# Cross-attention in one kernel: the transpose of the score maxima moved from the middle of a step to its end, the scores moved behind the output projection's first chunks

## What is computed

```python
q = split_heads(x @ Wq.T)            # 20 heads of 32
k = split_heads(ctx @ Wk.T)
v = split_heads(ctx @ Wv.T)
scores = einsum('bhsd,bhld->bhsl', q, k) / sqrt(32)
out = merge_heads(einsum('bhsl,bhld->bhsd', softmax(scores), v))
return out @ Wo.T + bo + x
```

## Time and profile before

| | |
|---|---|
| runs | 435.67 us median (434.54 to 435.75) |
| profiled execution | 436.16 us, of which the span in the profile is 434.4 us |
| TensorE matmul (PE) | busy 426.1 us, 98%, 2538 instructions |
| TensorE weight load (PEld) | 313.9 us, 72% |
| GpSimd (POOL) | 300.5 us, 69% |
| ScalarE (ACT) | 253.9 us, 58% |
| VectorE (DVE) | 232.7 us, 54% |
| chain of waits | PE 94%, POOL 2%, ACT 1%, DVE 1%, issue 1% |
| DMA | 72.68 MB, mean 167 GB/s |

### The profile page before, as it was taken

One profiled execution on the slowest core, in us unless ns is written; L12 is line 12 of the kernel. 1 busy time (PEld: TensorE's weight loads), 2 busy tenths in 40 slices (PEclk: granted clock), 3 DMA queues, 4 the chain that ended last, 5 costly groups with the idle time before them and its releaser, 6 DMA issues.

```text
span 434.4 us, 8258 instructions
## 1 busy us (share of the span) xinstructions
PE 426.1 (98%) x2538; PEld 313.9 (72%) x2538; DVE 232.7 (54%) x437; ACT 253.9 (58%) x509; POOL 300.5 (69%) x256
## 2 busy tenths in 40 slices
PE   8999999899999999999999999999999999999996
PEld 6977765677777777777777677777777677777675
DVE  0354766455545555555544555555554455555553
ACT  1737987657465755748464755757564755754510
POOL 8427799989568765959658674959658674955540
PEclk9999999899999999999999999999999999999999
DMA  8997545443455345543355335543355334444203
GB/s 288 359 351 230 203 135 196 146 146 127 145 191 174 122 151 205 205 146 123 135 186 190 123 130 206 204 166 123 125 195 189 124 121 150 157 157 146 75 24 121
DMA packets 39614, 72.68 MB, mean 167 GB/s; under 512 B 5024, under 2 KB 6176, under 8 KB 39584
## 3 DMA queue, kind: packets, MB, share of 16 engines
q1 hardware_dynamic: 28784, 52.62, 34.2%
q10 hardware_dynamic: 10800, 19.67, 14.0%
HBM read 28.81 MB, written 10.49 MB: 90 GB/s over the span
## 4 chain that ended last, share of the span: by engine, by line
PE 94%; POOL 2%; ACT 1%; DVE 1%; issue 1%; DMA 0%; POOLq 0%; ACTq 0%
PE ps_q L673 30%; PE ps_o L673 27%; PE ps_s L731 10%; PE ps_pv L738 7%; PE ps_m L717 5%; PE ps_den L743 4%; PE ps_o L656 2%; POOL p_lo L334 1%; PE ps_m L784 1%; PE ps_s L643 1%; PE ps_m L722 1%; PE ps_q L784 1%; PE ps_q L635 1%; DVE x_f L578 1%; PE ps_o L784 1%
## 5 line engine op out<-in xcount | busy, mean ns | idle before, releaser
L334 POOL TENSOR_TENSOR p_lo<-p_f,p_hi 77x512 f16<-77x512 f32 x160 | 183.2, 1166 | 99.8 <-ACT p_hi L432 97.8
L428 ACT ACTIVATE p_f<-ps_s 77x512 f32<-77x512 f32 x160 | 94.7, 592 | 47.6 <-PE ps_s L731 47.6
L548 DVE TENSOR_REDUCE mx<-ps_m 128x4 f32<-128x308 f32 x160 | 69.3, 475 | 57.7 <-PE ps_m L717 57.4
L432 ACT ACTIVATE p_hi<-ps_s 77x512 f16<-77x512 f32 x160 | 93.5, 584 | 3.0 <-PE ps_den L743 3.0
L541 DVE TENSOR_TENSOR q_lo<-ps_q,q_hi 128x512 fp32r<-128x512 f32 x40 | 27.7, 692 | 101.8 <-ACT q_hi L414 101.8
L673 PE MATMUL ps_q<-x_hi,wq_hi 128*128 128x512 f32 x200 | 79.4, 397 | 0.2 <-POOL wq_lo L348 0.2
L673 PE MATMUL ps_q<-x_lo,wq_hi 128*128 128x512 f32 x200 | 78.3, 391 | 0.0
L673 PE MATMUL ps_q<-x_hi,wq_lo 128*128 128x512 f32 x200 | 78.2, 391 | 0.0
L673 PE MATMUL ps_o<-attn_hi,wo_hi 128*128 128x512 f32 x170 | 70.0, 411 | 0.0
L673 PE MATMUL ps_o<-attn_hi,wo_lo 128*128 128x512 f32 x170 | 67.4, 397 | 0.0
L673 PE MATMUL ps_o<-attn_lo,wo_hi 128*128 128x512 f32 x170 | 67.4, 396 | 0.0
(11 more groups left out here) (105 smaller groups left out, 522.1 us busy)
## 6 DMA issues: line engine op xcount, KB each, us to landing
q_packed<-q_hi SPq DMA_DIRECT2D x80, 256.0 KB, 2.5
x_f<-in_x SPq DMA_DIRECT2D x40, 256.0 KB, 3.3
q_packed<-q_lo SPq DMA_DIRECT2D x40, 256.0 KB, 3.2
x_res<-in_x ACTq DMA_DIRECT2D x35, 256.0 KB, 2.7
out<-out_sb ACTq DMA_DIRECT2D x35, 256.0 KB, 2.6
wk_sb<-in_wk SPq DMA_DIRECT2D x8, 320.0 KB, 5.4
wv_sb<-in_wv SPq DMA_DIRECT2D x5, 512.0 KB, 5.9
wq_sb<-in_wq SPq DMA_DIRECT2D x5, 320.0 KB, 5.6
```

Of the source, the lines that this page charges most:

```text
L334: nc.gpsimd.tensor_tensor(p_lo[:, i, :], p_f[:, i, :], p_hi[:, i, :], ALU.subtract).then_inc(plo_done, 1)
L428: nc.scalar.activation(p_f[:, i, :], ps_s[i % 2][0:L, :], ACT.Exp, scale=SCALE).then_inc(pf_done, 1)
L432: nc.scalar.activation(p_hi[:, i, :], ps_s[i % 2][0:L, :], ACT.Exp, scale=SCALE).then_inc(phi_done, 1)
L548: nc.vector.tensor_reduce(mx[:, g % RS, :, tt], ps_m[tt % 2][:, 0:HG * L].rearrange("p (h k) -> p h k", k=L), AX_X, ALU.max).then_inc(max_ ...
```

## The change

On TensorE, in all steps behind the filling ones, the order within a step is another. Before: values, scores of heads 0 and 1, two maxima matmuls, output chunks 0 and 1, two maxima matmuls, score 2, output chunks 2 and 3, score 3, transpose of the maxima, output chunk 4, the five query chunks. After: values, two maxima matmuls, output chunks 0 and 1, two maxima matmuls, output chunk 2, scores 0 and 1, output chunks 3 and 4, score 2, query chunk 0, score 3, query chunks 1 to 4, transpose of the maxima. The filling steps stay as they were.

On ACT the copy of the maxima (`copy_max`), and on SP the transfer of them (`load_max`), move from the step that transposes them to the start of the next one. Nothing is added or removed.

```diff
@@ SP, step
-                if exists(shift(t, g, 1)[0]):
+                if exists(t) and not filling(*shift(t, g, -1)):
+                    load_max(t, g)
+                if filling(t, g) and exists(shift(t, g, 1)[0]):
                     load_max(*shift(t, g, 1))
@@ ACT, step
                 xt, (at, chunks) = x_split_at(t, g), attn_split_at(t, g)
+                if exists(t) and not filling(*shift(t, g, -1)):
+                    copy_max(t, g)
                 if exists(t):
                     exponentials(t, g, 0)
                     exponentials(t, g, 1)
...
-                if exists(shift(t, g, 1)[0]):
+                if filling(t, g) and exists(shift(t, g, 1)[0]):
                     copy_max(*shift(t, g, 1))
@@ PE, step
+                query = shift(t, g, 2)
                 values(last_t, last_g, batch(last_t))
-                if exists(t):
-                    scores(t, g, 0, batch(t))
-                    scores(t, g, 1, batch(t))
                 if exists(max_t):
                     max_scores(max_t, max_g, 0, batch(max_t))
                     max_scores(max_t, max_g, 1, batch(max_t))
...
+                if tiles:
+                    project_out(*tiles[0], (2,))
+                if exists(t):
+                    scores(t, g, 0, batch(t))
+                    scores(t, g, 1, batch(t))
+                if tiles:
+                    project_out(*tiles[0], (3, 4))
                 if exists(t):
                     scores(t, g, 2, batch(t))
-                if tiles:
-                    project_out(*tiles[0], (2, 3))
+                if exists(query[0]):
+                    project_q(*query, (0,))
+                for tile in tiles[1:]:
+                    project_out(*tile, (0, 1))
                 if exists(t):
                     scores(t, g, 3, batch(t))
+                if exists(query[0]):
+                    project_q(*query, range(1, G))
+                for tile in tiles[1:]:
+                    project_out(*tile, range(2, G))
                 if exists(max_t):
                     transpose_max(max_t, max_g)
-                if tiles:
-                    project_out(*tiles[0], (4,))
-                if exists(shift(t, g, 2)[0]):
-                    project_q(*shift(t, g, 2), range(G))
-                for tile in tiles[1:]:
-                    project_out(*tile, range(G))
```

## The result

The changed kernel takes 486.0 us (median of five runs, 482.99 to 496.52); the kernel before 435.67 us. The ratio is 1.1137, 95% interval 1.1106 to 1.1167: 11% slower. The forecast was slower, 472.5 us, range 456 to 496.

The account below looks back on a forecast made before the run. TensorE, busy throughout the steady part, was taken as the bound. To 436.16 us were added 24.3 (waits for the maxima), 7.1 and 3.0 (late query cast) and 2.0 (the end): 472.6, forecast as 472.5 us, range 456 to 496.

Parts of the forecast that it names:

- The wait per step: TensorE before the first scores: maxima at Lq+5.03, TensorE ready at Lq+4.27; 0.76 us in 32 steps, 24.3 us.
- Lq: Start of a step's last query matmul on TensorE, from which the forecast counts its times in us.
- The transpose: Transpose moved between last query matmul and value block: 4.1 us gain to 3.1 us cost possible, 0.0 taken.
- The late query cast: q_hi on ACT 1.2 us late behind group 0, 0.5 behind group 2, six times each: 7.1 and 3.0 us.
- GpSimd: p_lo 0.9 us late behind group 0, inside the 1.2 us already counted; attn_lo and x_lo covered by slack.
- The end: Last score step: three output chunks ahead of the first scores, most of their 2.05 us shows; 2.0 us.
- I take 2.0: Maxima's transfer issued behind the packing: 2.0 us from issue to landing, bounds 1.8 and 2.9 us.
- the clock case: Rival, 13 in 100: 12 longer waits (groups 1 and 3) drop TensorE's clock, 19 us more, 491 us.
- a landing of 2.6 us in every step: By the Trainium skill's rule the maxima never land before q_lo: 2.6 us after issue, sum 19 us higher, 492 us.
- The maxima land later still: Rival, 15 in 100: landing at 2.9 us, each step waits 1.7 us, 28.8 us more, 501 us.
- The maxima arrive in time: Rival, 10 in 100: request issued ahead of packing or landing quicker; GpSimd and ACT then bound, 451 us.
- Faster: Rival, 4 in 100: transpose vanishes in the turn and nobody waits, 432 us; needs a landing of 1.2 us or less.

Follow-up runs that it names:

- the run with waits of 3.3 us: Changed kernel with the scores left directly behind the value blocks, so only the transpose, its copy and its request are moved: 613.94 us, ratio 1.4122.
- two experiments: Changed kernel with the maxima's request ahead of the packing on SP: 454.19 us; kernel before with only the scores moved later: 453.5 us.
- The request one place ahead: Changed kernel with the maxima's request on SP behind the two q_hi packing requests but ahead of q_lo: 461.32 us, ratio 1.0598.
- six profiles: Two of the changed kernel (486.0, 489.02 us); request ahead of packing (454.19); one place ahead (461.32); first scores one chunk earlier (447.8); steps written out (491.93).

## Why the prediction was right, and where its size was off

**The bound and the mechanism.** Right. TensorE had been the bound, the loop through the query cast, SP's packing and the maxima's request is the bound now, and an earlier place of one request on SP removes it.

**The wait per step.** Predicted: request at Lq+2.99, landing 2.0 us, scores at Lq+5.03, wait 0.76 us. Measured: Lq+2.92, 2.10, Lq+5.06, 0.69. The step shown is 10.63 us, the ordinary ones are 10.5 to 10.8; 10.6 was said. The wait came out 0.07 us shorter because TensorE was ready at Lq+4.37 and not at Lq+4.27, so the step did not.

**The transpose.** Predicted 0.0. From the last query matmul to the value block are 0.43 us; before, 0.32 for that turn and 0.12 for the transpose elsewhere. The gain is 0.01 us per step at that turn.

**The late query cast.** Predicted 1.2 us behind group 0 and 0.5 behind group 2. The requests at 126.73 and 138.29 are 11.56 us apart (0.9 more than an ordinary step), those at 148.81 and 159.87 11.06 (0.4 more). So the two terms are 1.3 us together, not 1.7. Five steps, from 105.29 to 159.87, take 54.58 us, and the forecast's own terms give 54.6: that they agree so closely is in part luck, as the ordinary steps are a little longer than forecast.

**GpSimd.** p_lo was to be 0.9 us late behind group 0 and the wait to be covered: it is 0.80 (at 136.25 in the changed kernel) and the scores behind it still wait 0.58 us for the maxima, so it was covered. Once the queue is free it shows. So does attn_lo. The forecast had it 0.4 us ahead of its reader, but behind a wait of 0.76 us for the maxima; in the run with the request ahead of the packing TensorE waits 0.31 us for it behind group 0.

**The end.** Predicted 2.0 us. In the run with the request ahead of the packing the stretch from the last score step's value block to the end of the span is 30.8 us (421.29 to 452.1); before it was 28.6 (405.80 to 434.4): 2.2. In the profile of the changed kernel itself it is 32.6 (461.22 to 493.8), 4.0 more. There the granted clock was 0.57 from 471 to 475, behind an idle time of 2.20 us; the same idle time in the other run (430.06) left it at 1.00.

**The step that failed in size** is the landing as one number: "I take 2.0". A few long ones were named, at 10 us, in its bounds only, and are not in the sum. The sum without them, 472.5, is 13.5 us short of the median; the range held it also because it had been opened for the clock case and for a landing of 2.6 us in every step, neither of which came as it was told. In the profiled execution the 31 steps from the request at 94.23 to that at 453.15 take 358.9 us. With every step at its ordinary length (54.6 us per block, from the same trace) they would take about 338, and the kernel before took 31 x 9.815 = 304. So the waits I priced are 34 us there, as forecast (33.7 for 31 steps), and 21 us are the 7 slow landings, 2.9 us each in the mean. 1.8 of these are the later landing. The rest is in four of the seven (requests at 193.22, 311.87, 337.25 and 439.27), whose steps take 13.9 to 14.3 us: there the granted clock fell, to 0.50 to 0.75 over the 3 us behind the wait. Behind the three others TensorE had been idle for nearly as long (2.07 to 2.54 us, where the four had 2.19 to 2.69), the clock stayed at 1.00, and the steps take 12.6 to 13.4 us. The first of the four:

```profile
197.31 0.70 PE L735 MATMUL ps_s<-q_packed,k_packed 128*77 128x512 f32 x2 [2.61 <-DMA q_packed<-mxT]
...
198.51 0.63 PE L677 MATMUL ps_o<-attn_lo,wo_hi 128*128 128x512 f32 x1
```

A duration of 0.63 us goes with a granted clock of 0.50, as in the stretch of the earlier trace rows; at full clock it is 0.39. The fastest run, 482.99, would by this have about three slow landings, but it has no profile, so that is an estimate.

**The rivals.** "The maxima land later still": not in the median (2.1). The case with 2.6 us counted on a q_lo that lands 3.2 us behind its issue; in the changed kernel q_lo lands in 2.5 to 2.6, and the maxima just behind it (q_lo 115.27 plus 2.5, maxima 115.92 plus 2.1). "The waits cost the clock": not the ordinary ones, only behind four of the seven slow landings and at the end, and behind every wait of the run with waits of 3.3 us (granted clock 0.50 to 0.55 over the 3.5 us behind each). "The maxima arrive in time" (451 us) is what two experiments made of the kernel: 454.19 and 453.5. "Faster" had nothing: the transpose's place gives 0.01 us per step.

## What to carry to other kernels

When an operation is moved to save a tenth of a microsecond, follow its result to its reader through every in-order queue on the way: here the copy was ready at Lq+1.2 and the request still went out at Lq+2.9, because it stood in program order behind three requests that it did not depend on. A transfer that had slack has to be priced anew in its new place, at its issue behind the queue and at its landing behind what is under way, and with its spread: a median landing hides slow ones as long as there is slack, and once the transfer ends a wait in every step each slow one is paid in full and may cost the clock on top. The request one place ahead shows the edge: no cost in an ordinary step, and some 6 us for three slow landings. Late consumers of an in-order producer (here scores, exponentials, p_lo, attn_lo) should be checked in the steps where that engine has extra work, not in the ordinary step.

## What the runs showed that was not expected

- Slow landings of an 8 KB transfer, 3.6 to 4.1 us where 2.1 is usual, coincide in the changed kernel 7 times of 7 with a packet of the instruction queue behind their issue, and 25 ordinary ones never have one. Over six profiles all 26 landings above 3.0 us have such a packet between issue and landing; five that have one are not slow.
- With the same matmuls, waits of 3.4 us per step cost TensorE 66 us of busy time beyond the waits (492.6 against 426.1), at a mean granted clock of 0.863; waits of 0.7 us per step left the clock alone outside the slow landings. In between, the length of a single wait does not decide. In the changed kernel 2.07, 2.42 and 2.54 us left the clock at 1.00, and 2.19, 2.20, 2.61 and 2.69 us did not; an idle time of 2.20 us at the end lowered it there and not in the run with the request ahead of the packing.
- A transfer of 8 KB on ACT's queue takes 2.5 us when it is issued 0.15 us behind one of 256 KB on SP's, 1.8 us alone: the other queue spares the issue, not the landing.
